# Two convolution sums per word: 32-bit integer words in place of rounded halves

## The reference

```
x = x + block0(group_norm(x))
x = x + block1(group_norm(x))

block0(v): out  = conv3x3(sign(tile(v, 4)), sign(w1), groups=4)      # 256 channels, integer sums
           out  = relu(batchnorm1(out))
           out  = conv3x3(sign(out), sign(w2), groups=4)             # integer sums again
           out  = batchnorm2(out) * lambdas, summed over the 4 groups
           return relu(out + v)
block1(v): m    = resized mask;  mid = v * m
           att  = sigmoid(conv7x7([mean_c(mid), max_c(mid), m]))
           return relu(5 * instance_norm(mid * att))
```

## Time and profile before

| | |
|---|---|
| median of three runs | 318.55 us |
| span of the profiled execution, first to last instruction | 313.7 us |
| busy: TensorE, VectorE, ScalarE, GpSimd | 76%, 74%, 59%, 51% |

### The profile page before, as it was taken

The page is one execution under the profiler, slowest core; times in us unless marked ns, Lnnn a source line. Parts: engine busy times, 40 slices in busy tenths (PEclk is TensorE's granted clock), DMA queues, the critical chain, the costliest instruction groups (busy, mean ns, idle before and its releaser), DMA issues.

```text
span 313.7 us, 7083 instructions
## 1 busy us (share of the span) xinstructions
PE 239.8 (76%) x2742; PEld 152.2 (49%) x2742; DVE 233.7 (74%) x554; ACT 184.0 (59%) x223; POOL 159.5 (51%) x215
## 2 busy tenths in 40 slices
PE   7294798687888778888887697969696969676860
PEld 3252555345554445445554464546454645454550
DVE  3338754769886896979998969899968687758373
ACT  3434252384858584848486848675876768544221
POOL 3200410222423456576747656774768475938763
PEclk9858677699999999979999999999999999979885
DMA  7980000523015402631253314211611141131113
GB/s 202 310 270 3 0 2 0 155 65 106 2 54 135 124 27 78 174 95 64 86 155 101 104 58 131 80 51 55 154 54 53 74 137 53 53 117 38 51 53 154
DMA packets 11946, 28.86 MB, mean 92 GB/s; under 512 B 2285, under 2 KB 3565, under 8 KB 11757
## 3 DMA queue, kind: packets, MB, share of 16 engines
q1 hardware_dynamic: 11481, 28.13, 29.2%
q10 hardware_dynamic: 432, 0.29, 0.4%
HBM read 21.79 MB, written 6.61 MB: 91 GB/s over the span
## 4 chain that ended last, share of the span: by engine, by line
PE 31%; DVE 28%; issue 17%; ACT 15%; DMA 3%; POOL 3%; SPq 0%; ACTq 0%; DVEq 0%; POOLq 0%
PE big L892 15%; DVE big L614 9%; ACT round L465 5%; PE small L938 5%; ACT first L457 3%; DVE bnst L556 3%; DMA X<-in_x 3%; PE small L927 3%; ACT round L452 3%; ACT signs L437 3%; DVE gate L612 3%; DVE red L651 2%; DVE RD L627 2%; DVE S L618 2%; PE big L878 2%
## 5 line engine op out<-in xcount | busy, mean ns | idle before, releaser
L892 PE MATMUL big<-S,w2t 64*64 64x392 f16 x1152 | 59.3, 361 | 7.5 <-DVE S L618 7.5
L465 ACT ACTIVATE round<-big 128x784 f16<-128x784 f32 x32 | 26.1, 815 | 54.7 <-PE big L892 54.7
L878 PE MATMUL big<-E,w1t 64*128 64x392 f16 x576 | 55.8, 337 | 0.0
L927 PE MATMUL small<-cs,o 128*112 128x130 f32 x224 | 32.9, 287 | 27.2 <-DVE red L653 24.1
L627 DVE SCALAR_TENSOR_TENSOR RD<-round,big 128x784 f16<-128x784 f16 x32 | 30.7, 960 | 25.6 <-ACT round L465 25.6
L892 PEld LDWEIGHTS big<-S,w2t 64*64 64x64 f16 x1152 | 34.9, 115 | 27.1 <-DVE S L618 4.3
L927 PEld LDWEIGHTS small<-cs,o 128*112 128x112 f32 x224 | 26.4, 176 | 35.3 <-DVE red L653 27.4
L349 POOL TENSOR_TENSOR o<-o,mask_b 128x784 f32<-128x784 f32 x16 | 29.5, 1845 | 21.9 <-ACT o L484 21.9
L909 PE MATMUL big<-RD,wa 128*64 128x392 f16 x384 | 38.2, 352 | 1.3 <-DVE RD L627 1.3
L341 POOL TENSOR_TENSOR r<-ve,mhalf 128x1 f32<-128x1 f32 x16 | 8.9, 559 | 56.0 <-DVE ve L585 56.0
L556 DVE BATCH_NORM_STATS2 bnst<-X 128x6 f32<-128x392 f32 x64 | 32.8, 554 | 5.3 <-DMA X<-in_x 5.3
(11 more groups left out here) (119 smaller groups left out, 355.5 us busy)
## 6 DMA issues: line engine op xcount, KB each, us to landing
X<-in_x SPq DMA_DIRECT2D x16, 392.0 KB, 6.4
mask_b<-mask_rows SPq DMA_DIRECT2D x32, 196.0 KB, 3.5
out<-o SPq DMA_DIRECT2D x16, 392.0 KB, 2.3
att_b<-attention_rows SPq DMA_DIRECT2D x28, 196.0 KB, 3.9
o<-in_w SPq DMA_DIRECT2D x3, 576.0 KB, 9.7
o<-in_masks SPq DMA_DIRECT2D x1, 512.0 KB, 11.0
cs<-in_cst SPq DMA_DIRECT2D x1, 385.0 KB, 11.1
o<-in_sel SPq DMA_DIRECT2D x1, 343.0 KB
```

The lines of the kernel that those rows point to most:

```text
L465: act.activation(round2[:, hh, :], sums(f"c2_{hh}"), ACT.Copy, bias=BASE - MID).then_inc(rounded2, 1)
L878: mm = pe.matmul(acc[:, LOW + HALF * hh:LOW + HALF * (hh + 1)], w1t[64 * hh:64 * hh + 64, s, q * P:(q + 1) * P], window(RH * hh, s // 3, s ...
L892: mm = pe.matmul(acc[64 * q:64 * q + 64, LOW + HALF * r:LOW + HALF * (r + 1)], w2t[64 * r:64 * r + 64, s, 64 * q:64 * q + 64], window(RH * ...
L927: mm = pe.matmul(small[1 - n % 2][0:CP, at:at + P + 2], o[:, t, CP * j:CP * (j + 1)], cs[:, K_ID:K_ID + P + 2], start=True, stop=True)
```

## The change

The factor is now chosen so that a PSUM element times a scale is a 32-bit integer whose upper 16 bits are one sum and whose lower 16 bits stand for the other.

- `words1` and `words2`: one ScalarE pass each takes the scaled sum out of PSUM into an int32 tile, `word1` or `word2`, in place of two passes. `round1`, `first`, `round2` are gone.
- `gates`: L612's comparison reads the upper halves (int16, every second 16-bit element of `word1`, SBUF). L614 is gone. L618's comparison reads the lower halves (uint16 in SBUF) and `gate0` (SBUF) where it read PSUM and `gate0`. It has a new wait for `gate0`, since no instruction stands between them now.
- `split_sums`: VectorE's instruction with two tensors (SBUF and PSUM) becomes a `tensor_scalar` on the lower halves of `word2` (SBUF).
- `high_half`: the upper halves of `word2` go to fp16 in `RD[..., 0, :]` by a GpSimd `tensor_copy`, where ScalarE had L472. It waits for `worded2`, and for the mix that last read this part of `RD`.
- Waits of TensorE: join waits for `worded1` (ScalarE) in place of `gated`, conv1(t, 1) for `worded2` in place of `split`. mix still waits for both halves of `split`, and for `whole2`, which GpSimd now raises.
- One small VectorE instruction (`thr_low`, 128 x 2) in the preparation.

The core of the diff:

```diff
@@ gpsimd
+            def high_half(t, hh):
+                if not has(t):
+                    return
+                pool.wait_ge(worded2, t * 2 + hh + 1)
+                wait(pool, y_done, (t - 2) * 2 + hh + 1)
+                pool.tensor_copy(RD[:, t % 2, hh, 0, :], high2[:, hh, :]).then_inc(whole2, 1)
...
+            high_half(0, 0)
             for k in range(1, NT):
+                high_half(k - 1, 1)
...
                 last_sum(k - 5)
+                high_half(k, 0)
@@ scalar
-            def round_sums1(t, q):
+            def words1(t, q):
                 act.wait_ge(conv1_done, t * 2 + q + 1)
-                wait(act, whole1, t * 2 + q)
-                act.activation(round1[:, :], sums(f"c1_{q}"), ACT.Copy, bias=ROUND, scale=1.0 / IMG)\
-                   .then_inc(rounded1, 1)
-                act.wait_ge(rounded1, t * 2 + q + 1)
-                wait(act, parted1, t * 2 + q - 1)
-                wait(act, gated0, t * 2 + q - 1)
-                act.activation(first[:, q, :], round1[:, :], ACT.Copy, bias=-ROUND).then_inc(whole1, 1)
+                wait(act, gated, t * 2 + q - 1)
+                act.activation(word1[:, q, :], sums(f"c1_{q}"), ACT.Copy, bias=WORD / 2, scale=WORD / IMG)\
+                   .then_inc(worded1, 1)
...
-                act.activation(round2[:, hh, :], sums(f"c2_{hh}"), ACT.Copy, bias=BASE - MID).then_inc(rounded2, 1)
-            def move_back(t, hh):
...
-                act.activation(RD[:, t % 2, hh, 0, :], round2[:, hh, :], ACT.Copy, bias=-BASE).then_inc(whole2, 1)
+                act.activation(word2[:, hh, :], sums(f"c2_{hh}"), ACT.Copy, bias=LIFT, scale=WORD)\
+                   .then_inc(worded2, 1)
@@ vector
             def gates(t, q):
-                dve.wait_ge(whole1, t * 2 + q + 1)
-                dve.tensor_scalar(gate0[:, q, :], first[:, q, :], thr[:, q:q + 1], GATE, ALU.is_gt, ALU.mult)\
+                dve.wait_ge(worded1, t * 2 + q + 1)
+                dve.tensor_scalar(gate0[:, q, :], high1[:, q, :], thr[:, q:q + 1], GATE, ALU.is_gt, ALU.mult)\
                    .then_inc(gated0, 1)
-                dve.scalar_tensor_tensor(sums(f"c1_{q}"), first[:, q, :], -IMG, sums(f"c1_{q}"), ALU.mult, ALU.add)\
-                   .then_inc(parted1, 1)
-                dve.wait_ge(parted1, t * 2 + q + 1)
+                if t == 0:
+                    dve.wait_ge(thr_ready, 1)
+                dve.wait_ge(gated0, t * 2 + q + 1)
                 wait(dve, conv2_done, t * 2 - 2)
                 dve.scalar_tensor_tensor(inside(S2[:, t % 2, q, :]),
-                                         sums(f"c1_{q}").rearrange("p (h w) -> p h w", w=W), thr[:, q:q + 1],
+                                         low1[:, q, :].rearrange("p (h w) -> p h w", w=W), thr_low[:, q:q + 1],
                                          gate0[:, q, :].rearrange("p (h w) -> p h w", w=W), ALU.is_gt, ALU.add)\
...
-                    dve.scalar_tensor_tensor(RD[:, t % 2, hh, 1, :], round2[:, hh, :], BASE, sums(f"c2_{hh}"),
-                                             ALU.subtract, ALU.subtract).then_inc(split, 1)
+                    dve.tensor_scalar(RD[:, t % 2, hh, 1, :], low2[:, hh, :], LIFT, 1.0 / UNIT,
+                                      ALU.subtract, ALU.mult).then_inc(split, 1)
@@ tensor
             def join(t):
-                wait(pe, gated, 2 * t - 1)
+                wait(pe, worded1, 2 * t - 1)
             def conv1(t, q):
                 if q == 1:
-                    wait(pe, split, 2 * t - 1)
+                    wait(pe, worded2, 2 * t - 1)
```

More of the change, by code:

```diff
@@ L13 @@
 F16 = mybir.dt.float16
+I32 = mybir.dt.int32
+I16 = mybir.dt.int16
+U16 = mybir.dt.uint16
 P = 128
@@ L32 @@
 ROUND = 1.5 * 2.0 ** 23
+WORD = 65536.0
 IMG = 2046.0
 GATE = 1024.0
-BASE = 1324.0
-MID = 144.0 / GATE
+UNIT = WORD / GATE
+LIFT = 368.0 * UNIT
 REACH = 600.0
@@ L96, in build @@
         E = sb("E", [P, 2, PAD], F16)
-        round1 = sb("round1", [P, HW], F32)
-        first = sb("first", [P, 2, HW], F16)
-        round2 = sb("round2", [P, 2, HW], F16)
+        word1 = sb("word1", [P, 2, HW], I32)
+        word2 = sb("word2", [P, 2, HW], I32)
         gate0 = sb("gate0", [P, 2, HW], F16)
@@ L147, in build @@
         thr = sb("thr", [P, 2], F32)
+        thr_low = sb("thr_low", [P, 2], F32)
         flip_row = sb("flip_row", [P, P], F16)
@@ L186, in sums @@
             return big[SLOT[name]][:, at:at + halves * HALF]
+        low1, high1 = (word1[:, :, :].bitcast(dt).rearrange("p q (n two) -> p q n two", two=2)[:, :, :, h]
+                       for h, dt in ((0, U16), (1, I16)))
+        low2, high2 = (word2[:, :, :].bitcast(dt).rearrange("p q (n two) -> p q n two", two=2)[:, :, :, h]
+                       for h, dt in ((0, U16), (1, I16)))
         def inside(padded):
@@ L216, in build @@
         signed, joined, packed = sem("signed"), sem("joined"), sem("packed")
-        conv1_done, rounded1, whole1, parted1 = sem("conv1_done"), sem("rounded1"), sem("whole1"), sem("parted1")
+        conv1_done, worded1, thr_ready = sem("conv1_done"), sem("worded1"), sem("thr_ready")
         gated0, gated = sem("gated0"), sem("gated")
-        conv2_done, rounded2, whole2, split = sem("conv2_done"), sem("rounded2"), sem("whole2"), sem("split")
+        conv2_done, worded2, whole2, split = sem("conv2_done"), sem("worded2"), sem("whole2"), sem("split")
         y_done, y_added, block_relu, x1_ready = (
@@ L411, in _ @@
                 last_sum(k - 5)
+                high_half(k, 0)
+            high_half(15, 1)
             power2(14)
@@ L517, in _ @@
             for q in range(2):
-                round_sums1(0, q)
+                words1(0, q)
             pack_signs(1)
-            round_sums2(0, 0)
-            move_back(0, 0)
+            words2(0, 0)
             for k in range(1, NT):
-                round_sums2(k - 1, 1)
-                move_back(k - 1, 1)
+                words2(k - 1, 1)
                 sign_x(k + 1)
-                round_sums1(k, 0)
+                words1(k, 0)
                 normalise2(k - 2)
-                round_sums1(k, 1)
+                words1(k, 1)
                 relu_block(k - 1)
@@ L532, in _ @@
                 last_relu(k - 5)
-                round_sums2(k, 0)
-                move_back(k, 0)
+                words2(k, 0)
                 sigmoid(k - 2)
-            round_sums2(15, 1)
-            move_back(15, 1)
+            words2(15, 1)
             normalise2(14)
@@ L689, in thresholds @@
                 link(dve.scalar_tensor_tensor(thr[:, :], near[:, :], 0.5, at_near[:, :], ALU.add, ALU.subtract))
+                dve.tensor_scalar(thr_low[:, :], thr[:, :], WORD / IMG, WORD / 2, ALU.mult, ALU.add)\
+                   .then_inc(thr_ready, 1)
             def sign_weights():
```

10 lines of the change are left out of this document (3 added, 7 removed).

## The result

The changed kernel takes **322.87 us** (median of 20 runs, 319.58 to 326.02), the kernel before 318.36 us beside it (20 runs, 314.62 to 320.36): ratio 1.0129, interval 1.0095 to 1.0162. It is slower by 1.3%. The forecast was 317 us, "within 1%"; the time lies in the range (301 to 334), and the sign was wrong.

The account below looks back on a forecast made before the run. No engine near full; the short iteration's chain runs over VectorE's full queue. Loop +2.4, iterations 1 to 4 -2.7, start -1.1, end +0.6 give -0.8 us, thus 317.8, forecast as 317 us; range 301 to 334.

Parts of the forecast that it names:

- rival C: VectorE's 16-bit halves don't run two at a time: four instructions take 1.03 for 0.6 us; effects cancel within 2 us.
- rival B: GpSimd's queue becomes the bound, with casts near 1.85 us: 330 to 340 us; chance 0.28.
- The door: SBUF ports shared by VectorE and GpSimd: each shuts the other out for whole instructions; VectorE uses it about 4.5 us a tile.
- rival A: Sharing SBUF ports costs little, VectorE's 2.2 us saving counts: 300 to 304 us; chance 0.27.
- The long iteration: Loop iteration where attention matmuls follow conv2: 15.4 us forecast, against 16.05 before.
- The short iteration: Loop iteration without attention matmuls after conv2: 15.0 to 15.8, say 15.3 us, against 14.17; VectorE's gain lost to port waits.
- the race's ends: Short iteration, L341 and L343 against VectorE's comparisons for the SBUF ports: make_u ends at 12.2 to 13.0 us.
- The loop as a whole: Five pairs of iterations, k = 5 to 15: +2.4 us, with bounds +0.9 to +4.9.
- Iterations 1 to 4: Iterations where attend or last_sum are not there yet: -0.9, -0.9, -0.6, -0.3, together -2.7 us.
- The start: Up to the first conv2: -2.3 us; a later clash of second comparison and add_x gives 1.2 back: -1.1.
- Up to 4 us less: If the shared SBUF ports are idle in more handovers than assumed, the walk gives up to 4 us less; hence 317 us.
- my own case: The predictor's main forecast of 317 us: chance 0.45, own range 311 to 322 us.

Follow-up runs that it names:

- the kernel with the moved cast: Changed kernel with GpSimd's cast of (k-1, 1) queued behind the two small instructions L351 and L353: 321.39 us, 1.0117 of the kernel before.
- Comparisons free: Changed kernel with the first comparison's gate written to PSUM, splits still reading SBUF, casts on GpSimd: 299.6 us, 0.9454 of the kernel before.
- no door: Changed kernel with gate written to PSUM and split's low half read from PSUM, casts on GpSimd: 300.71 us, 0.9461 of the kernel before.
- the two with both remedies: Changed kernel with casts on ScalarE and gate in PSUM, with the split from PSUM (300.16 us) or from SBUF (301.87 us).

## Why the prediction was wrong, step by step

- **ScalarE's pass, VectorE's prices, the cast: right.** int32 out of PSUM takes 0.808 and 0.819 us. Comparison and split of 16-bit halves take 0.57 and 0.52 us alone, forecast 0.6, so rival C is out. The cast takes 0.84 us, forecast 1.0; 1.85 us, rival B's price, is out. Comparisons with both operands in SBUF keep 1.04 us.
- **The door: right, and rival A is out.** A VectorE instruction with its operands in SBUF and a GpSimd instruction shut each other out; without it the spread of all four groups is gone, and the time with it. The rule of the Trainium skill that the prediction named agrees with this.
- **The long iteration: right.** Forecast 15.4 us, measured 15.3 in the mean of five (15.12, 15.61, 14.81, 15.75, 15.28).
- **The short iteration: this step failed.** Forecast 15.3 us with 15.8 as the bound, measured 16.5 in the mean (16.81, 16.31, 17.36, 15.94, 16.18). The order of events was right up to the comparison: the second split ends 6.65 us after conv2's start (forecast 6.5), the casts end at 8.1 (8.4). Then three things were wrong. First, I took a value between the race's ends, but it has one outcome here: casts and comparison come to the door at the same time, and both small instructions are held. make_u ends at 13.15 us in three of the five, beyond the worst I had allowed (13.0) and 0.6 us beyond the middle. Second, in the other two it ends at 14.0 us. There the statistics of a batch of four tiles put one more small instruction (L345, 1.04 us at 141.76) in front of L351. The walk was made in an iteration that has none, and before the change GpSimd's idle time hid most of it (14.34 us for 14.17). TensorE waits longest there:

```profile
147.66 2.81 PE L936 MATMUL small<-cs,o 128*112 128x130 f32 x14 [3.73 <-POOL o L359]
```

  Together this is 0.9 us an iteration. Third, I let TensorE run at its full clock after any wait. From the turn's start to conv2 it takes 2.44 us where the clock is up (the long iterations), and 2.74 to 3.30 us, 2.98 in the mean, in these five: 0.5 us. The forecast had about 2.7 for this part, so against the forecast the clock adds 0.3. The causes are read from the timelines; that the clock's part is on the path is shown by an experiment for the kernel with the moved cast, and only in one profile for this one.
- **The loop as a whole:** +6.8 us (159.17 against 152.41) for +2.4. I had also taken five times 30.22 us, 151.1, for the loop before. That is 1.3 us too little, above all because one conv2 in it runs at the lower level and takes 1.6 us more:

```profile
134.85 0.48 PE L927 MATMUL small<-cs,o 128*112 128x130 f32 x2 [1.74 <-DVE red L653]
135.26 4.89 PE L892 MATMUL big<-S,w2t 64*64 64x392 f16 x72
```

- **Iterations 1 to 4:** -1.5 us, forecast -2.7. One by one they are -1.7, +0.9, +0.6 and -1.3 us, forecast -0.9, -0.9, -0.6 and -0.3: only the sum is near, by luck.
- **The start:** +0.8 us, forecast -1.1. The first conv2 does come 2.66 us sooner (30.70 for 33.36, forecast -2.3), but the band matmuls that follow then run at a granted clock of 0.50 for 5.4 us, see the second window above. Before, the same stretch is

```profile
36.80:39.60 2.80, 2.80 (x29) 2.80 (x28) 2.56 (x10) 1.45 (x2) 2.14 (x7) 1.00 0.00 0
```

  at 1.00, and the second conv2 starts at 39.65 us before and at 39.66 after: the band matmuls take 5.43 us for 2.94, so 2.5 of the 2.66 us went to the clock. Why it is low there, no run shows. The clash of the second comparison with the first add_x, forecast at 1.2 us, is there: L625 takes 2.49 us at 56.19.
- **The end:** +0.2 us, forecast +0.6.
- **"Up to 4 us less".** The sum gave 317.8 us, and I took 317 for a reason that no row carried. The parts together give +6.2 us and so do the spans; the sum had -0.8, and 4.4 of the difference is the loop.
- **The chances.** I gave my own case 0.04 above 321.8 us and let "slower" rest on rival B. It came from my own mechanism. In this chain what follows a longer wait (a slower clock, a missed turn at the door) cost on top of it, so the range should have reached further up than down.
- **B in part:** GpSimd did become the engine on the chain (3% to 26%), yet not by the casts' work but by where it stands: doubled and free of the door, it costs 4.0 us.

What stays open: what bounds the five fastest versions. Comparisons free, casts on ScalarE, no door, and the two with both remedies lie at 299.6 to 301.9 us, with overlapping intervals, and TensorE busy 79% and 80% of the span in the first two. Open as well is how much the second cast's place costs: with it moved, another clash took the gain. The fastest of the changed kernel's relatives is thus three lines away (the gate into PSUM, 299.6 us), or one engine away (the cast on ScalarE, 299.72 us): either beats the kernel before by 5.5%.

## What to carry to other kernels

When work moves from PSUM into SBUF, or to GpSimd, list every VectorE instruction that from then on has only SBUF operands, and lay them in time beside GpSimd's queue: the price can be set by the smallest GpSimd instruction that someone waits for, here one of 0.19 us. Walk through an iteration of every kind, also the one with an extra small instruction. An operand left in PSUM, even at half the speed (1.03 for 0.57 us), can be the cheaper one. And where a step leaves TensorE waiting longer, here 0.9 to 3.7 us in front of the turn, price the work behind the wait at both of its clock levels (the turn 2.1 or up to 3.4 us, conv2 3.25 or 4.9).

## What the runs showed of the hardware that was not expected

- An instruction of one element a partition on GpSimd is shut out like a large one: L353 took 1006 ns for 189, L351 981 for 548. L353's counterpart took 189 to 192 ns, 16 of 16, in every version without the comparisons at the door.
- Not every VectorE instruction that has only SBUF operands is caught: the statistics instruction L563, with one fp32 tensor, takes 514 to 570 ns in all its 96 executions in the changed kernel, also beside GpSimd's sums (at 170.46 a pair of it takes 1.02 us inside the sum of 170.07 to 172.24).
- TensorE came down to the lower clock level after single waits of a few us, in kernels that keep it busy otherwise, and the length of the wait doesn't tell when. In the changed kernel the turn was slowed after each of the five waits of 2.87 to 3.73 us in the short iterations of the loop, but not after one of 2.44 us (289.36). After waits of 2.34 us conv2 was slowed in eight cases of ten. After 2.11 and 2.12 us it was not in one kernel, and after 2.12 us it was in another. In the kernel before it was slowed once after 1.74 us, where twelve other such waits (1.72 to 1.75 us) were followed by 3.25 us. One conv2 cost up to 1.65 us by it.
- Earlier work can lose nearly all of its lead to the clock: 2.66 us gained at 30.70 us were gone at 39.66 us.
- ScalarE writes int32 from PSUM in 0.81 us, as long as fp32 (0.80); VectorE reads every second 16-bit element of 784 in 0.52 to 0.57 us, where a contiguous fp16 tensor took 0.42 and instructions with an operand in PSUM 0.96 to 1.04.
